# Identity matmuls on TensorE at the phase borders of a one-core transformer kernel

## The reference, cut to what matters

```python
x = x + _L0_attn_ref(_layernorm(x), Wq, bq, Wk, bk, Wv, bv, Wo, bo, prior_lambda)
# then x + ffn_ref(_layernorm(x)), where ffn_ref is, for l in (0, 1):
def _layer(x, wqkv, qs, ksc, wo, lg, lb, w1, b1, w2, b2):
    h = shift_token(x)
    q, k, v = jnp.split(h @ wqkv, 3, axis=-1)          # to heads
    q = l2norm(q) * qs
    k = l2norm(k) * ksc
    q, k = rotary_xpos(q, k)
    x = x + local_attention(q, k, v) @ wo
    h = shift_token(x)
    h = (h - mu) / jnp.sqrt(var + 1e-05) * lg + lb
    a, g = jnp.split(h @ w1 + b1, 2, axis=-1)
    return x + (a * gelu(g)) @ w2 + b2
```

## Time and profile before

| | |
|---|---|
| median of three runs | 5754.36 us (5754.29 to 5756.47) |
| profiled execution | 5754.29 us, span 5752.5 us |
| PE busy | 5589.2 us (97% of the span) |
| DVE busy | 4806.7 us (84%) |
| ACT busy | 3795.6 us (66%) |
| mean granted TensorE clock | 0.989 of full |

### The profile page before, as it was taken

The page is one execution under the profiler, slowest core; times in us unless marked ns, Lnnn a source line. Parts: engine busy times, 40 slices in busy tenths (PEclk is TensorE's granted clock), DMA queues, the critical chain, the costliest instruction groups (busy, mean ns, idle before and its releaser), DMA issues. The chain is left out here.

```text
span 5752.5 us, 160685 instructions
## 1 busy us (share of the span) xinstructions
PE 5589.2 (97%) x66780; PEld 3580.7 (62%) x66908; DVE 4806.7 (84%) x9926; ACT 3795.6 (66%) x6471; POOL 2219.5 (39%) x1811
## 2 busy tenths in 40 slices
PE   8999999999999999999998999999999999999999
PEld 3544454444444444444553888888787788888787
DVE  8988898888888888889995888888676888888676
ACT  4777776777767777677775777777333677777333
POOL 3011102211012121030001889998111889988222
PEclk9999999999999999999999999999999999999999
DMA  3111111111111111111111544554100455545111
GB/s 97 28 40 31 44 28 37 41 41 41 31 31 40 44 45 37 32 44 43 28 22 30 117 113 112 115 115 113 33 12 15 108 114 117 113 113 119 52 53 48
DMA packets 270856, 350.52 MB, mean 61 GB/s; under 512 B 45664, under 2 KB 173488, under 8 KB 270128
## 3 DMA queue, kind: packets, MB, share of 16 engines
q1 hardware_dynamic: 270128, 340.25, 24.6%
HBM read 103.90 MB, written 41.94 MB: 25 GB/s over the span
## 5 line engine op out<-in xcount | busy, mean ns | idle before, releaser
L668 ACT ACTIVATE a_pr<-a_w 128x1024 f32<-128x1024 f32 x2048 | 1990.6, 1022 | 668.0 <-PE a_w L544 556.0
L804 DVE TENSOR_REDUCE a_mx<-a_b 128x1 f32<-128x512 f32 x2658 | 1713.5, 685 | 184.0 <-PE a_b L525 181.8
L525 PE MATMUL a_b<-a_kp,a_qp 96*32 96x512 bf16 x16200 | 1469.1, 381 | 38.7 <-DVE a_mx L802 20.2
L544 PE MATMUL a_w<-a_qp,a_kp 99*32 99x512 bf16 x16384 | 1276.2, 380 | 3.6 <-ACT a_pr L668 3.0
L802 DVE CUSTOM_DVE_ANT_0 a_junk<-a_b,a_gw 128x512 bf16<-128x512 f32 x1392 | 953.4, 685 | 179.3 <-PE a_b L525 127.0
L574 PE MATMUL a_po<-a_pr,a_v 128*17 128x512 f32 x8192 | 1079.3, 593 | 0.4 <-ACT a_pr L668 0.4
L525 PEld LDWEIGHTS a_b<-a_kp,a_qp 96*32 96x32 bf16 x16200 | 508.8, 96 | 860.9 <-issue 346.6
L1680 POOL TENSOR_TENSOR l_p<-l_p,l_rc 128x512 f32<-128x512 f32 (+1 forms) x512 | 721.8, 1438 | 28.3 <-DVE l_rc L1578 28.1
L544 PEld LDWEIGHTS a_w<-a_qp,a_kp 99*32 99x32 bf16 x16384 | 491.2, 97 | 387.3 <-ACT a_pr L668 36.3
L1325 PE MATMUL l_G<-l_wqkv,l_hT 128*128 128x512 f32 x2304 | 618.0, 413 | 29.6 <-DVE l_hT L1521 23.1
L1468 ACT ACTIVATE l_p<-l_S,l_nm 128x256 f32<-128x256 f32 (+1 forms) x1024 | 471.8, 471 | 202.7 <-DVE l_nm L1570 202.5
(11 more groups left out here) (236 smaller groups left out, 8833.5 us busy)
## 6 DMA issues: line engine op xcount, KB each, us to landing
l_qs<-l_qT SPq DMA_DIRECT2D x512, 128.0 KB, 2.3
l_kh<-l_kT SPq DMA_DIRECT2D x512, 128.0 KB, 2.4
l_kl<-l_kT SPq DMA_DIRECT2D x256, 128.0 KB, 2.4
l_tab<-in_rotary SPq DMA_DIRECT2D x128, 128.0 KB, 2.4
a_xc<-in_x SPq DMA_DIRECT2D x28, 512.0 KB, 4.1
q_parts<-raw SPq DMA_DIRECT2D x32, 384.0 KB, 2.6
k_parts<-raw SPq DMA_DIRECT2D x32, 384.0 KB, 2.5
a_qp<-q_parts SPq DMA_DIRECT2D x64, 192.0 KB, 3.7
```

Source lines behind the costliest of these rows:

```text
L525: m = eng.matmul(bk[32 * r:32 * r + 32, :], qp[s][0:96, o:o + 32], kp[s][0:96, c * 512:c * 512 + 512], start=True, stop=True)
L544: m = eng.matmul(wide[u][32 * r:32 * r + 32, c * 512:c * 512 + 512], kp[s][0:99, o:o + 32], qp[s][0:99, u * 1024 + c * 512:u * 1024 + c * ...
L668: eng.activation(pr[(2 * n + u) % NP][:, :], wide[u][:, :], ACT.Exp, scale=0.25).then_inc(s_exp[u], 1)
L804: t = eng.tensor_reduce(mx[g % 2][:, qb, c:c + 1], banks[i], X, ALU.max)
```

## The change

A helper `keep_busy` issues a number of f32 matmuls of the identity with itself, 128 columns each, into a PSUM bank that nothing reads at that time. It is called at these places: in `attention` between the waits for `s_ones` and `s_kones` (16 matmuls) and after the last `out_project` (22); in `local_layer` ahead of `qkv(n, 0)` for n = 0, 1, 2, 3 (12, 12, 12, 7) and behind the last iteration (8); in `feed_forward` ahead of the first transposes (6), and, in the first of the two, behind the last group (8). The waits that come with them are for semaphores that the same engine's earlier work or the earlier phases have already brought.

```diff
+def keep_busy(eng, bank, ident, times):
+
+    for _ in range(times):
+        eng.matmul(bank[:, 0:128], ident[:, :], ident[:, :], start=True, stop=True, skip_group_check=True)
...
         m.then_inc(full, 1)
         pe.wait_ge(s_ones, 1)
+        keep_busy(eng, po, ident, 16)
         pe.wait_ge(s_kones, 1)
         for n in range(-LEAD, NS + 1):
...
             out_project(("out_project", NB - 1, w0))
+        pe.wait_ge(s_osb, NB * HA)
+        keep_busy(eng, po, ident, 22)
...
 SHIFT = 16 * 3
+BUSY = (12, 12, 12, 7)
...
         x_T(0)
         for n in range(NT + 4):
+            keep_busy(eng, R[1], ident, BUSY[n] if n < len(BUSY) else 0)
             on(qkv, n, 0)
...
                 on(pv, n - 3, pair)
+        pe.wait_ge(s_pc, 4 * NT)
+        keep_busy(eng, R[1], ident, 8)
...
+        pe.wait_ge(s_ident, 16)
+        keep_busy(eng, Y[1], ident, 6)
         for i in range(4):
             turned(0, i)
...
                 for i in TURNED[j] if g + 1 < NG else ():
                     turned(g + 1, i)
+        if not last:
+            keep_busy(eng, F[0], ident, 8)
```

## The result

| | before | changed |
|---|---|---|
| median, measured side by side | 5754.7 us (5754.29 to 5757.03, 8 runs) | 5739.13 us (5737.54 to 5743.09, 8 runs) |
| profiled execution | 5754.29, span 5752.5 | 5738.69, span 5736.9 |
| mean granted clock | 0.989 | 0.995 |
| PE busy | 5589.2 us | 5600.0 us |

The ratio is 0.9973, 95% interval 0.9962 to 0.9984: 15.6 us faster, with an interval of about 6 us to either side. The kernel is faster beyond the noise; the ratio itself is beyond the 0.2% that the prediction asked for, the near end of its interval (0.16%) isn't. The forecast was 5741.4.

A forecast was written before the change was run, and what follows sets the result against it. PE, busy 97% of the span, bounds the kernel; a full clock could return about 63 us at most. The terms -1.8 - 5.6 - 4.8 + 0 - 0.8 = -13.0 take 5754.4 to 5741.4; forecast's range 5733 to 5749, overall 5731 to 5755.

The forecast's parts named there:

- Price: Everywhere: one added f32 matmul of 128 columns costs 0.22 us at full clock, 0.43 at half; bounds 0.21 and 0.57.
- rivals of price: All places: if f32 weight loads don't hide, a matmul costs up to 0.57 us; +34 us, 5788; chance 0.05.
- matmuls that don't hold the clock: All places: the clock falls where it fell, added matmuls behind the fall cost 0.43 us; +8, 5762; chance 0.13.
- Attention: Attention's opening: 16 matmuls win 0.9 us at DVE's eighth bank and 0.9 at the 99 to 104 fall; -1.8 us.
- The three drops: Inside attention: three similar half-clock stretches of some 6 us, untouched by the change, shift with time; -0.8 us in all.
- Border to local_layer 0: Between attention and local_layer 0: the 22 make PE end last, at 3142.9 instead of about 3142.4; +0.5 us.
- The sign that the prediction gave for it: Local_layer 0's first instruction about 5.4 us behind the last out_project, 0.5 more than before less its own shift.
- Local openings: First four iterations of both local layers: full clock wins 8.2 and 6.4 us, less 2.1 and 1.6 for remaining falls.
- Feed-forward borders: Both feed-forward openings: PE last costs 0.7 us, one-column products don't hold the clock, 0.7 won; 0 for each border.
- the right bound, -3.4: Each feed-forward border: 4.08 us of DVE waiting less 0.7 of cost, if full clock lasts through the one-column products.
- The sum: Whole kernel: -1.8 - 5.6 - 4.8 + 0 - 0.8 = -13.0 us, giving 5741.4.
- everything holds: Clock stays full through local openings, bias columns and most drops inside attention; -26 us, 5728; chance 0.1.

The follow-up runs named there:

- doubled openings: Changed kernel with 24, 24, 24, 14 instead of 12, 12, 12, 7 matmuls in the openings of both local layers; 5747.37 us.
- two added groups: Changed kernel plus 9 identity matmuls at the start of iteration 64 and 5 ahead of tile 63's scores, in each local layer; 5738.14 us.
- late weights: Kernel with 9 and 5 more matmuls in the last local iterations, plus SP holding the next weights' load until tile 63's scores are made; 5739.17 us.

## Why the prediction was right, and where it was not

**Price.** 0.22 us was predicted and 0.23 measured, in rows of 16, 22 and 24. The rivals of price and of matmuls that don't hold the clock are both out. The doubled openings show what too many cost: 9.2 us in the two openings, 8.2 in the median.

**Attention.** -1.8 and -0.8 were predicted, together -2.6, and the profiled execution has -2.55; but its parts were wrong. The three drops did not shrink (0.52 after, 0.53 before, in the first), nor did a fourth that the prediction left out (0.50 from 3107 to 3117 before, 0.53 from 3104 to 3115 after). The first scores were late by their DMA in this trace, 47.53 and not 46.5, and DVE's eighth bank started at 52.35 where it was at 52.56: 0.2 us won there, not 0.9. What made up for most of it is the fall near 99 us, which is absent in this trace (1.00, not 0.66). And the trace of the changed kernel is a lucky one: in eleven traces with the 16 the last out_project starts between 3132.96 and 3135.79, middle 3134.89; in three without them at 3135.78, 3136.21 and 3137.25. The three earliest are those in which the fall near 99 us is absent; in the other eight it came back. The 16 are worth about 1.3 us at attention's end, by the middle ones, and with only them no gain shows at the kernel's end, in a median that couldn't tell 1.3 us. That -2.6 was met is luck.

**Border to local_layer 0.** +0.5 predicted, +0.83 measured. The sign that the prediction gave for it, the new phase 5.4 us behind the last out_project, doesn't fit its own rows: the earlier trace rows have 5.60 without the 22, and it is 6.43 with them. That the 22 do something for the first iteration was taken for granted; without them the time is the same.

**Local openings.** -6.1 and -4.8 predicted, -6.30 and -4.85 measured. The sums hold, one of the reasons does not. Iterations 0, 1 and 2 gave 2.1, 1.0 and 2.0 in layer 0, where 2.2, 0.9 and 2.2 had been read. For falls still to come 2.1 was taken off, but no fall came (1.00 throughout). What was too large instead was iteration 3: 1.25 won up to the rotation of tile 4, not 2.9. Two errors met, which is luck. DVE's waits ahead of the rotations of tiles 0 and 3 stayed at about 1.0 us, where the prediction expected 0.5 or less.

**Feed-forward borders.** This step failed, and by a sign that the prediction itself had named: L1864 was to take 8 us or more of its 9.4, and takes 5.55. The cost was right: PE is the last engine at the barrier, 0.85 us against 0.7. The gain was put at 0.7 a border and was about 4. The step read the ten microseconds at 0.50 as "one-column products don't hold the clock". The row shows only that they don't raise it once it is down. With the 6 ahead of the transposes the clock was full when they began, and most of the 44 records ran before it fell: windows of the changed kernel in and behind its first one-column stage read 1.00 and 0.50.

```profile
4032.00:4036.00 4.00, 4.00 (x38) 4.00 (x37) 3.08 (x4) 2.56 (x4) 0.00 (x0) 1.00 0.36 89
4037.00:4043.00 6.00, 5.65 (x15) 4.52 (x16) 4.25 (x19) 0.69 (x1) 1.01 (x1) 0.50 0.61 171
```

That the clock falls all the same was right, as it did in every trace that has the 6 and the bias products as they were; that it falls soon was not. The fall came 2.3 to 4.5 us behind the first one-column product. Without the 6 the 44 records took 8.6 us. The text had the right bound, -3.4 (-3.0 and -3.3 were measured, with the cost), and chose the wrong end.

**Last iterations of local_layer 0.** A stretch that the prediction left out, because the change doesn't touch it, took back 4.4 us in the trace. The wait of 2.27 us was in the kernel before as well; whether the clock falls behind it depends on more than its length. The kernel before had this fall in layer 1 (the stretch 5304 to 5310 reads 0.72) and not in layer 0; the changed kernel has it the other way round. In eleven traces that leave this place open, the fall at the first wait of layer 0 is there in seven. They are just those that have the 12, 12, 12 and 7: the rotation of tile 63 is at 3982.8 to 3986.1 in them, and at 3987.8 to 3990.8 in the other four (the kernel before, only the 16, only the feed-forward borders, the doubled openings). Less the 0.85 where the 8 stand, the stretch lost 1.1 to 4.8 us in the seven, 2.7 in the middle. So in layer 0 this loss goes with the change and is not bad luck of one trace; that it comes from the time to which the change moves the wait is likely and not shown. In layer 1 it doesn't divide so: of the same seven, three have the fall at that wait and four don't. The two added groups take it away in all three kernels that have them. A part is left that no run explains: in four traces with no fall ahead of it, l_kl still landed 1.1 to 1.4 us later than before. The late weights did not mend it, and its cause stays open.

**The sum.** -13.0 was predicted and -15.6 measured, and that they are so near is in part luck: 6.6 us more from the two feed-forwards, 4.4 lost and 0.9 won in the last iterations, the rest within 0.35 a term. The rival "everything holds" (-26) failed on the drops in attention, on the clock that still falls in the one-column products, and on the last iterations.

## What to carry to other kernels

Work that only keeps TensorE busy pays in a wait ahead of products for which other engines wait. Here the 12, 12, 12 and 7 ahead of the broad qkv products won 11.1 us in the two openings, the largest part, and six matmuls ahead of one-column products, which don't raise the clock by themselves, about 3 us a layer. It gives little or nothing where further such work stands behind it, as the first 12 behind the 22 do, and at borders where it makes TensorE the last at a barrier. Size it to the wait by its price in the trace, since what goes over is paid, more than half of it here. And when a change moves the whole program by a few microseconds, look at the open waits that it didn't touch: a fall of the clock behind them comes or stays away. In the changed kernel's trace one such stretch took back 4.4 us, more than either feed-forward gave.

## What was not expected of the hardware

- One-column f32 products behind full clock: 44 records in 5.3 to 7.3 us in the traces that have the 6, where at 0.50 they take 9.4 us. PE counts as busy in either case.
- f32 transposes of 128 columns hold the granted clock as matmuls of the same size do: 1.00 in the same stretches, 2.78 against 2.84 us for 24 records.
- The same wait of 2.27 us ahead of the same instructions is followed by half clock in some traces and not in others: eight transposes behind it take 1.91 or 1.04 us.
